# A gated delta layer on one core: v turned by VectorE and transfers, the residual's product kept in PSUM, and new queue orders

## The chip, the cores and the metric

The kernel runs on one core of one Trainium2 chip. The metric is the device time of one execution in microseconds (us). The engines run side by side, each from its own queue in its own order: TensorE (PE in the profile, its weight loads PEld), VectorE (DVE), ScalarE (ACT), GpSimd (POOL) and SyncE (SP), which issues every transfer (DMA). They wait for one another by semaphores. Matrix products land in PSUM, here eight banks of 128x512 f32; everything else an engine works on lies in SBUF.

## The reference

All of it is f32. A layer norm, a gated delta rule over 16 sequences of 256 tokens and 32 heads of 64, a residual, and a small feed-forward part:

```python
qkvz = (hidden_states @ w_qkvz.T)            # then q, k, v through a causal conv of 4 taps
g = -jnp.exp(A_log) * jax.nn.softplus(a + dt_bias);  beta = jax.nn.sigmoid(b)
q = _l2norm(q) * DK ** (-0.5);  k = _l2norm(k)
def step(Sstate, xs):
    q_t, k_t, v_t, g_t, b_t = xs
    Sstate = Sstate * jnp.exp(g_t)[..., None, None]
    kv = jnp.einsum('bhk,bhkv->bhv', k_t, Sstate)
    delta = (v_t - kv) * b_t[..., None]
    Sstate = Sstate + k_t[..., :, None] * delta[..., None, :]
    o_t = jnp.einsum('bhk,bhkv->bhv', q_t, Sstate)
    return (Sstate, o_t)
o = o * lax.rsqrt(var + EPS) * norm_weight * jax.nn.sigmoid(z)
x = x + _layernorm(o.reshape(Bsz, Sl, VDIM) @ w_out.T)
x = x + _layernorm((jax.nn.silu(gate) * up) @ w_down.T)
```

## The kernel before

Three stages follow each other: the first norms and the gates (up to about 110 us), the delta rule, and the feed-forward part (from about 3000 us).

The delta rule is cut into 64 steps: 8 groups of 4 heads by 8 spans of 512 tokens. A step holds 16 chunks of 64x64 (G = 16) for each of the two halves of 64 partitions. Its recurrence is written chunk by chunk: within a chunk the triangular system is inverted, between chunks a state of 64x64 is carried, over 4 chunks a sequence (c = 0 to 3); every step starts with an empty state. The inverse is built from 16x16 blocks on VectorE (`substitute`, 15 columns, each a product and a subtraction), joined on TensorE to 32 (`join16_inner`, `join16_outer`) and to 64 (`join_inner`, `join_outer`).

The steps run in a software pipeline four deep. The program is written out in turns: in turn t an engine works on the steps `s[0]` = t, `s[1]` = t - 1, `s[2]` = t - 2 and `s[3]` = t - 3, and the function `turn` of each engine is an order written out by hand. There are 67 turns; the pace of the stage is the length of a turn. Engines take a step at different depths: what GpSimd and SyncE call `s[3]` is not the step that TensorE calls `s[3]`.

What TensorE does for a step, in the names of the code:

- `project(m, s, bank)`: 8 projections into one of the banks 0 to 3 (2 k, 2 q, 2 v, 2 z), each two products of 128x128 by 128x512; `xT` is the input, in two buffers. ScalarE and VectorE take the taps out of the bank (`first_tap`, `tap_product`, `conv`); GpSimd adds q's taps (`add_tap`).
- `k_tokens` and `v_tokens` (both through `tokens`, line 1266): k and v are turned from channels by tokens to tokens by channels, as products with a unit matrix, a half of the step in each call. `scale_k` and `scale_v` (lines 1073 and 1077) take the result out of PSUM and scale it into `kt` and `v_r`.
- `scores`: k against k and q, four calls. `matrices` (lines 1089 and 1090) multiplies them with the decays into `a_mat` and `p_t`.
- for each chunk c: `key_state` (the state against k, line 1332), `residual` on VectorE (lines 1100 and 1103: the product with `b_eg` goes to `rhs`, then v minus it to `rhs`), `solve` (line 1342), `delta_out` on ScalarE (line 894), `advance` (line 1352), `new_state` on VectorE (line 1113), and `output` (lines 1365 and 1367). `decay_state` (line 1106) prepares `s_dec` for `new_state`.
- `sum_squares`, then after VectorE's `combine` and `gated` the output product `project_out`, added up by `accumulate`.

SyncE's transfers in a turn: `units_out` (16x16 blocks of `a_mat` to DRAM, 4 transfers of 32x16x32), `load_gates`, `units_in` (back as `a_un`, one row a block), then after `turn_units` on ScalarE `z_out` and `z_back`, `x_out` and `x_back`, and `load_x` for `xT`. A transfer that waits holds up those behind it in SyncE's queue.

The banks: before, each use of the banks 0 to 3 is written out as a number; bank 4 holds the chunk recurrence, bank 5 the joins, banks 6 and 7 the output.

Of the kernel before, what the change touches and what calls it, by code (L numbers as in the profile page):

```python
# [18 lines left out]
def gated_delta_sandwich(nc, x, w_qkvz, w_ba, conv_w, a_log, dt_bias, norm_w, w_out, w_gu, w_dn,  # L19
                         c_ident, c_masks, c_ones, c_eye, out):  # L20
    F32 = mybir.dt.float32
    ALU = mybir.AluOpType
# [3 lines left out]
    P = 128  # L26
# [4 lines left out]
    TB = 512  # L31
# [23 lines left out]
    with ctx:  # L55
# [37 lines left out]
        xT = [sb(f"xT{i}", [P, HT, TB]) for i in range(2)]  # L93
# [31 lines left out]
        x_row = sb("x_row", [P, G, C])  # L125
        p16 = sb("p16", [P, G, W2])
# [15 lines left out]
        class Own:  # L142


            def __init__(self, eng, s):
                self.eng, self.s, self.n = eng, s, 0
# [9 lines left out]
            def turn(self):  # L156
                if self.n:
                    self.need(self.n)
                    self.eng.sem_clear(self.s)
                    self.n = 0  # L160
# [17 lines left out]
        x_T_in = [sem(f"x_T_in{i}") for i in range(2)]  # L178
# [6 lines left out]
        with ExitStack() as s1:  # L185
# [45 lines left out]
            with nc.Block() as block:  # L231
                @block.sync
                def _(sync):
# [51 lines left out]
                    sp.dma_start(xT[0][:, :, :].rearrange("p h t -> p (h t)"), xT_d[0]).then_inc(x_T_in[0], 16)  # L285
# [253 lines left out]

        def flat(t):  # L540
            return t[:, :, :].rearrange("p a b -> p (a b)")

        wgu = [[flat(xT[0]), flat(xT[1])], [flat(w_two[1])[:, 0:INTER], flat(w_two[1])[:, INTER:2 * INTER]]]
# [16 lines left out]
        with ExitStack() as s2:  # L560
# [5 lines left out]
            abs_done = sem2("abs_done")  # L566
            cols_done = sem2("cols_done")
            comb_done = {i: sem2(f"comb_done{i}") for i in (0, 1,)}
            conv_done = {i: sem2(f"conv_done{i}") for i in (0, 1, 4, 5,)}
            deca_done = sem2("deca_done")  # L570
            delta_done = {i: sem2(f"delta_done{i}") for i in (0, 1, 2, 3,)}
# [9 lines left out]
            mats_done = {i: sem2(f"mats_done{i}") for i in (0, 1,)}  # L581
# [8 lines left out]
            qg_done = {i: sem2(f"qg_done{i}") for i in (1,)}  # L590
            rhs_done = {i: sem2(f"rhs_done{i}") for i in (1, 2, 3,)}
            rk_done = sem2("rk_done")
            score_full = {i: sem2(f"score_full{i}") for i in (0, 1, 2,)}
            sdec_done = {i: sem2(f"sdec_done{i}") for i in (2,)}
# [4 lines left out]
            sub_done = {i: sem2(f"sub_done{i}") for i in (0, 1, 2, 3, 4, 5,)}  # L599
            sumk_done = {i: sem2(f"sumk_done{i}") for i in (0,)}  # L600
            tap_added = {i: sem2(f"tap_added{i}") for i in (0, 1, 2, 3, 4, 5,)}
            tap_done = {i: sem2(f"tap_done{i}") for i in (0, 1, 2, 4, 5,)}
            tap_prod = {i: sem2(f"tap_prod{i}") for i in (3, 4, 5,)}
            usq_done = {i: sem2(f"usq_done{i}") for i in (0, 1,)}
            var_log = {i: sem2(f"var_log{i}") for i in (0, 1,)}
            vr_done = {i: sem2(f"vr_done{i}") for i in (0,)}
            vtok_full = {i: sem2(f"vtok_full{i}") for i in (0, 1,)}
# [6 lines left out]
            z_clamped = {i: sem2(f"z_clamped{i}") for i in (1,)}  # L614
# [1172 lines left out]
```

## Time and profile before

| | us |
|---|---|
| median of 3 runs | 3383.96 |
| lowest, highest | 3382.12, 3391.8 |
| the profiled execution | 3383.12 |
| its span, first to last instruction | 3381.2 |
| PE busy in the span | 3202.0 |
| DVE busy | 2463.0 |
| ACT busy | 1749.5 |
| POOL busy | 1094.8 |

The page is read from the top: which engine is busy for nearly the whole span, then whether that share is even over it. The groups of instructions by line tell what such an engine does and what ended its idle time. A row of the timeline has a start, a duration, the instruction, and in brackets the idle time ahead of it with what ended it. Starts of neighbouring rows tell what a block of pipelined instructions costs; its duration is a little longer, since blocks overlap.

### The profile page before, as it was taken

The page shows a single profiled execution, that of the slowest core. Times are in us where ns is not written, and L with a number is a line of the kernel's source. Part 1 is how long each engine was busy: PE and PEld are TensorE (multiplying, and loading weights), DVE is VectorE, ACT ScalarE, POOL GpSimd, SP SyncE. Part 2 cuts the span into 40 slices and gives each one's busy share as a digit, 9 for nine tenths or more (in the row PEclk, how much of TensorE's full clock was granted, in tenths as well). Part 3 has the DMA queues.
Part 4 walks back from the last instruction along what each step waited for, and adds up shares of the span by engine and source line. Part 5 has one row for each costly group of instructions (what it writes and reads, how often), then busy time and mean ns, then how long its engine had stood idle before and what let it go on. Part 6 is the DMA issues. An engine that isn't in the chain of part 4 may idle for free. (4 is left out here: it accounts for less than half of the span.)

```text
span 3381.2 us, 116979 instructions
## 1 busy us (share of the span) xinstructions
PE 3202.0 (95%) x51008; PEld 2181.8 (65%) x51008; DVE 2463.0 (73%) x5802; ACT 1749.5 (52%) x3306; POOL 1094.8 (32%) x904
## 2 busy tenths in 40 slices
PE   6799999999999999999999999999999999879998
PEld 3466666666666666666666666666666666645554
DVE  6677777777777777777777777777777777645554
ACT  5455555555555555555555555555555555433332
POOL 1443443333343443333343443333343343200000
PEclk8899999999999999999999999999999999989999
DMA  5233233222333222222332223222232223200000
GB/s 144 57 53 64 47 51 52 44 63 52 53 53 68 44 50 53 58 49 52 52 68 51 46 49 62 51 49 50 53 68 53 48 47 52 56 33 25 19 19 19
DMA packets 757483, 175.67 MB, mean 52 GB/s; under 512 B 707568, under 2 KB 728432, under 8 KB 755824
## 3 DMA queue, kind: packets, MB, share of 16 engines
q1 hardware_dynamic: 756976, 168.19, 26.2%
q8 instruction: 406, 6.65, 0.8%
q14 instruction: 101, 0.83, 0.1%
HBM read 120.13 MB, written 39.58 MB: 47 GB/s over the span
## 5 line engine op out<-in xcount | busy, mean ns | idle before, releaser
L1257 PE MATMUL bank<-xT,w_sb 128*128 128x512 f32 x2048 | 1018.7, 621 | 9.9 <-PEq L506 5.2
L741 POOL TENSOR_TENSOR kq<-kq,product 128x510 f32<-128x510 f32 (+2 forms) x384 | 445.0, 1165 | 882.8 <-ACT kq L829 597.2
L1257 PEld LDWEIGHTS bank<-xT,w_sb 128*128 128x128 f32 x2048 | 349.5, 190 | 295.5 <-issue 251.7
L1042 DVE SCALAR_TENSOR_TENSOR kq<-bank,cw,kq 128x510 f32<-128x510 f32 (+2 forms) x384 | 286.7, 747 | 163.0 <-ACT kq L829 149.3
L729 POOL TENSOR_TENSOR dec_a<-gcrow,gcb 128x1024 f32<-128x1024 f32 x64 | 121.8, 1903 | 832.2 <-DMA gcb<-gcb_d 832.2
L1042 DVE SCALAR_TENSOR_TENSOR v_c<-bank,cw,v_c 128x510 f32<-128x510 f32 (+2 forms) x384 | 285.3, 743 | 9.0
L1060 DVE TENSOR_TENSOR x_un<-x_un,prod_un 128x15 f32<-128x15 f32 (+7 forms) x960 | 258.3, 269 | 32.9
L1056 DVE TENSOR_TENSOR prod_un<-a_un,x_un 128x15 f32<-128x15 f32 (+7 forms) x960 | 255.8, 266 | 30.1 <-DMA a_un<-a_d 3.2
L1285 PE MATMUL bank<-kq 64*64 64x128 f32 x4096 | 270.3, 271 | 4.4 <-DVE v_c L1042 2.1
L1389 PE MATMUL bank<-wo,u_sq 128*128 128x256 f32 x1024 | 260.9, 399 | 3.5 <-DVE u_sq L1125 3.5
L835 ACT ACTIVATE product<-bank,cw 128x512 f32<-128x512 f32 x384 | 246.7, 703 | 0.0
L1367 PEld LDWEIGHTS bank<-p_t,delta 64*64 64x64 f32 x4096 | 215.1, 136 | 47.0 <-issue 47.0
L1367 PE MATMUL bank<-p_t,delta 64*64 64x64 f32 x4096 | 243.3, 220 | 0.0
L1365 PEld LDWEIGHTS bank<-q_g,state 64*64 64x64 f32 x3072 | 179.6, 134 | 95.4 <-issue 95.4
L1285 PEld LDWEIGHTS bank<-kq 64*64 64x64 f32 x4096 | 229.8, 133 | 7.6 <-issue 7.6
L894 ACT COPY delta<-bank 128x256 f32<-128x256 f32 x256 | 94.7, 370 | 244.3 <-PE bank L1342 244.3
L1389 PEld LDWEIGHTS bank<-wo,u_sq 128*128 128x128 f32 x1024 | 188.1, 193 | 34.4 <-DVE u_sq L1125 4.3
L1365 PE MATMUL bank<-q_g,state 64*64 64x64 f32 x3072 | 205.8, 226 | 1.1 <-ACT delta L894 1.1
L829 ACT ACTIVATE kq<-bank,cw 128x512 f32<-128x512 f32 x256 | 170.0, 690 | 62.4 <-PE bank L1257 62.4
L1342 PE MATMUL bank<-rhs,z_t 64*64 64x64 f32 x3072 | 128.3, 222 | 72.6 <-DVE rhs L1103 72.6
L1342 PEld LDWEIGHTS bank<-rhs,z_t 64*64 64x64 f32 x3072 | 107.3, 135 | 127.0 <-issue 127.0
L1089 DVE TENSOR_TENSOR a_mat<-bank,dec_a 128x256 f32<-128x256 f32 x256 | 106.4, 415 | 107.2 <-PE bank L1285 106.9
(170 smaller groups left out, 6004.7 us busy)
## 6 DMA issues: line engine op xcount, KB each, us to landing
xT<-xT_d SPq DMA_DIRECT2D x64, 512.0 KB, 3.8
gcrow<-gcrow_d SPq DMA_DIRECT2D x128, 256.0 KB, 4.5
a_d<-a_mat SPq DMA_DIRECT2D x256, 64.0 KB, 2.1
z_t<-z_d SPq DMA_DIRECT2D x256, 64.0 KB, 2.5
w_sb<-in_w_qkvz SPq DMA_DIRECT2D x8, 1024.0 KB, 5.9
x_un<-eye_un SPq DMA_DIRECT2D x64, 128.0 KB, 3.7
a_un<-a_d SPq DMA_DIRECT2D x64, 128.0 KB, 4.7
z_d<-t_un SPq DMA_DIRECT2D x64, 128.0 KB, 3.0
```

Of the source, the lines that this page charges most:

```text
L741: nc.gpsimd.tensor_tensor(t[:, :, d:SEQ], t[:, :, d:SEQ], prod[:, :, 0:SEQ - d], ALU.add).then_inc(tap_added[i], 1)
L829: ins = nc.scalar.activation(dst, bank[:, :], ACT.Identity, scale=cw_two[m.grp % 2][:, s * TAPS + TAPS - 1:s * TAPS + TAPS])
L835: ins = nc.scalar.activation(products[i % 4], bank[:, :], ACT.Identity, scale=cw_two[m.grp % 2][:, w:w + 1])
L1042: ins = nc.vector.scalar_tensor_tensor(t[:, :, d:SEQ], src[:, :, 0:SEQ - d], cw_two[m.grp % 2][:, w:w + 1], t[:, :, d:SEQ], ALU.mult, ALU.add)
L1056: own.need(own.mark(nc.vector.tensor_tensor(prod, a_un[:, j + 1:B, j:j + 1].broadcast_to([P, rows, wid]), x_un[:, j:j + 1, 0:wid].broadcas ...
L1060: ins = nc.vector.tensor_tensor(rest, rest, prod, ALU.subtract)
L1257: ins = nc.tensor.matmul(bank[:, :], w_two[m.grp % 2][:, h, s * P:(s + 1) * P], xT[m.par][:, h, :], start=(h == 0), stop=(h == HT - 1))
L1285: ins = nc.tensor.matmul(bank[half, i * P:(i + 1) * P], kq[half, k, s // 2, t0:t0 + C], kq[half, k:q + 1:q - k, s // 2, t0:t0 + C], start= ...
L1342: ins = nc.tensor.matmul(banks[4][half, 256 + i * C:256 + (i + 1) * C], z_t[m.par][half, g, :], rhs[half, i, :] if c else v_r[m.par][half, ...
L1365: nc.tensor.matmul(o, state[c % 2][half, i, :], q_g[m.par][half, g, :], start=True, stop=False)
L1367: ins = nc.tensor.matmul(o, delta[half, i, :], p_t[m.par][half, g, :], start=(c == 0), stop=True)
L1389: ins = nc.tensor.matmul(bank[:, t * HID:(t + 1) * HID], u_sq[:, a, (2 * k + t) * P:(2 * k + t + 1) * P], wo[m.grp % 2][:, a, :], start=(a ...
```

## The change

1. `v_tokens` is gone from TensorE. `turn_v` on VectorE transposes 32x32 blocks of v from `v_c` into a new buffer `v_x`, a half of the step in each call; eight transfers (`v_turned`) lay the blocks out in `v_r`; `scale_v` then works in place on `v_r` in SBUF. It runs a turn later than before.
2. `residual` writes its product back into its PSUM bank and subtracts from there.
3. `substitute` is called column by column, 15 parts in place of 6, with other work between them; it starts in one turn and ends in the next.
4. `xT` has one buffer in place of two (`product` takes over as the buffer of a weight in the last stage). `decay_state` now always signals.
5. The banks 0 to 3 are used in a ring that turns by two each step.
6. Every engine's order in a turn is new.

```diff
-        xT = [sb(f"xT{i}", [P, HT, TB]) for i in range(2)]
+        xT = sb("xT", [P, HT, TB])
+        v_x = sb("v_x", [P, G, C])
+        def ring(m, place):
+            return banks[(18 * m.off + place) % 4]
...
+                    def v_turned(m):
+                        for h in range(2):
+                            for f in range(2):
+                                for t in range(2):
+                                    r, q = D * h + W2 * t, D * h + W2 * f
+                                    sp.dma_start(v_r[m.par][r:r + W2, :, W2 * f:W2 * f + W2], v_x[q:q + W2, :, W2 * t:W2 * t + W2]) \
+                                        .then_inc(v_f_in, 16)
...
+                    def turn_v(m, a):
+                        ins = nc.vector.transpose(v_x[:, a * GP:(a + 1) * GP, :].rearrange("p g c -> p (g c)"), v_c[:, a, :])
+                        if a in vx_done:
+                            ins.then_inc(vx_done[a], 1)
...
-                    def scale_v(m, a, bank):
+                    def scale_v(m, a):
                         g = slice(a * GP, (a + 1) * GP)
-                        ins = nc.vector.tensor_tensor(v_r[m.par][:, g, :], bank[:, :].rearrange("p (g c) -> p g c", c=C), col(br[:, g]).broadcast_to([P, GP, C]), ALU.mult)
+                        ins = nc.vector.tensor_tensor(v_r[m.par][:, g, :], v_r[m.par][:, a * GP:(a + 1) * GP, :], col(br[:, g]).broadcast_to([P, GP, C]), ALU.mult)
...
                     def residual(m, c):
-                        own.need(own.mark(nc.vector.tensor_tensor(
-                            rhs[:, :, :], banks[4][:, 0:256].rearrange("p (a j) -> p a j", j=C),
-                            col(b_eg[m.par][:, c:G:NCH]).broadcast_to(four), ALU.mult)))
-                        nc.vector.tensor_tensor(rhs[:, :, :], grp(v_r[m.par], c), rhs[:, :, :], ALU.subtract).then_inc(rhs_done[c], 1)
+                        ks = banks[4][:, 0:256].rearrange("p (a j) -> p a j", j=C)
+                        own.need(own.mark(nc.vector.tensor_tensor(ks, ks, col(b_eg[m.par][:, c:G:NCH]).broadcast_to(four), ALU.mult)))
+                        nc.vector.tensor_tensor(rhs[:, :, :], grp(v_r[m.par], c), ks, ALU.subtract).then_inc(rhs_done[c], 1)
...
-                    def v_tokens(m, a, bank):
-                        ins = tokens(v_c[:, :, :], a, bank)
-                        ins.then_inc(vtok_full[a], 1)
```

What stands where now is shown for three places. Some semaphores are shown under the name of an earlier stage that used the same one.

TensorE, the part of a turn from `sum_squares` to `advance` of chunk 0; before, with `v_tokens` as `bank<-masks,v_c` and one early projection:

```order
L1382 MATMUL bank1<-u_sq,ones 128x512 [waits sq_added1]
L1382 MATMUL bank2<-u_sq,ones 128x512 [waits sq_added0]
L1314 MATMUL bank5<-z_t1,a_mat1 32x32 [waits z16_done]
L1314 MATMUL bank5<-z_t1,a_mat1 32x32 x31
L1266 MATMUL bank3<-masks,v_c 64x64 [waits mats_done1]
L1266 MATMUL bank3<-masks,v_c 64x64 x15
L1266 MATMUL bank0<-masks,v_c 64x64 [waits mats_done0]
L1266 MATMUL bank0<-masks,v_c 64x64 x15
L1323 MATMUL bank5<-p1,x_top 32x32 [waits p1_done,xtop_done]
L1323 MATMUL bank5<-p1,x_top 32x32 x31
L1257 MATMUL bank1<-xT1,w_sb1 128x512 [waits x_T_in1,comb_done1]
L1257 MATMUL bank1<-xT1,w_sb1 128x512
```

And now:

```order
L1355 MATMUL bank5<-p16,x_row 48x32 x31
L1432 MATMUL bank2<-u_sq,ones 128x512 [waits sq_added0]
L1310 MATMUL bank3<-xT,w_sb1 128x512 [waits x_T_in,mats_done2]
L1310 MATMUL bank3<-xT,w_sb1 128x512
L1310 MATMUL bank0<-xT,w_sb1 128x512 [waits mats_done0]
L1310 MATMUL bank0<-xT,w_sb1 128x512
L1364 MATMUL bank5<-z_t1,a_mat1 32x32 [waits z16_done]
L1364 MATMUL bank5<-z_t1,a_mat1 32x32 x31
L1439 MATMUL bank1<-wo1,u_sq 128x256 [waits og_done0]
L1439 MATMUL bank1<-wo1,u_sq 128x256 x3
L1373 MATMUL bank5<-p1,x_top 32x32 [waits p1_done,xtop_done]
```

The 32 products of `v_tokens` are gone, and two projections of the next step (`bank<-xT,w_sb`) stand between the joins, where they wait for nothing that is computed in the turn but the matrices and the input.

VectorE, ahead of the second `residual`; before, the columns 9 to 14 of the substitution stand in one piece (the last five rows of it here) ahead of it:

```order
L1056 TENSOR_TENSOR prod_un<-a_un,x_un 128x28 [waits soft]
L1060 TENSOR_TENSOR x_un<-x_un,prod_un 128x2x14 [waits soft]
L1056 TENSOR_TENSOR prod_un<-a_un,x_un 128x15 [waits soft]
L1060 TENSOR_TENSOR x_un<-x_un,prod_un 128x15 [waits soft]
L1100 TENSOR_TENSOR rhs<-bank4,b_eg1 128x256 [waits ks_full2]
L1103 TENSOR_TENSOR rhs<-v_r1,rhs 128x256 [waits soft]
```

And now:

```order
L1149 TENSOR_TENSOR state<-bank,s_dec 128x256 [waits st_full1,sdec_done1]
L1116 TENSOR_TENSOR v_r<-v_r,cols 128x512 [waits v_f_in]
L1089 TENSOR_TENSOR prod_un<-a_un,x_un 128x15 [waits tok_ready]
L1093 TENSOR_TENSOR x_un<-x_un,prod_un 128x15 [waits tok_ready]
L1144 TENSOR_TENSOR s_dec<-state,e_end 128x256 [waits state_done1]
L1140 TENSOR_TENSOR bank<-bank,b_eg 128x256 [waits ks_full2]
L1141 TENSOR_TENSOR rhs<-v_r,bank 128x256 [waits tok_ready]
```

Between `new_state` of chunk 1 and the second `residual` only one column, one `scale_v` and one `decay_state` are left.

SyncE, one turn; before:

```order
L671 DMA a_d<-a_mat1 32x16x32 [waits mats_done0]
L671 DMA a_d<-a_mat1 32x16x32 x3
L659 DMA gcrow<-gcrow_d 64x2x512 [waits qg_done1]
L659 DMA gcrow<-gcrow_d 64x2x512
L662 DMA gcb<-gcb_d 128x32
L676 DMA a_un<-a_d 128x16x16 [waits a_d_out]
L679 DMA z_d<-t_un 128x16x16 [waits alpha_done]
L687 DMA x_d<-x_un 64x16x16
L684 DMA z_t1<-z_d 32x16x32 [waits z_d_out]
```

And now:

```order
L669 DMA gcrow<-gcrow_d 64x2x512 [waits qg_done1]
L669 DMA gcrow<-gcrow_d 64x2x512
L672 DMA gcb<-gcb_d 128x32
L681 DMA a_d<-a_mat 32x16x32 [waits mats_done0]
L681 DMA a_d<-a_mat 32x16x32 x3
L686 DMA a_un<-a_d 128x16x16 [waits a_d_out]
L709 DMA v_r<-v_x 32x16x32 [waits vx_done1]
L709 DMA v_r<-v_x 32x16x32 x7
L697 DMA x_d<-x_un 64x16x16 [waits sub_done14]
L689 DMA z_d<-t_un 128x16x16 [waits gc_ready]
L694 DMA z_t<-z_d 32x16x32 [waits z_d_out]
```

The gates' three transfers now go ahead of the blocks of `a_mat`, v's eight stand behind the load of `a_un`, and the two results of the substitution behind those.

## Rows read from the trace of the kernel before

**Rows 1.** The page: the span and each engine's busy time.

```profile
span 3381.2 us, 116979 instructions
PE 3202.0 (95%) x51008; PEld 2181.8 (65%) x51008; DVE 2463.0 (73%) x5802; ACT 1749.5 (52%) x3306; POOL 1094.8 (32%) x904
```

**Rows 2.** Busy time by windows: stretch, length, PE, PEld, DVE, ACT, POOL, clock, DMA.

```profile
200.00:2600.00 2400.00, 2335.86 (x41365) 1624.82 (x41361) 1845.83 (x4300) 1318.78 (x2478) 910.32 (x751) 1.00 0.29 54
```

**Rows 3.** PE's groups by line: count, busy us, mean ns, idle before and releaser.

```profile
L1266 PE MATMUL bank<-masks,v_c 64*64 64x64 f32 x4096 | 134.0, 220 | 0.7 <-issue 0.6
L1342 PE MATMUL bank<-rhs,z_t 64*64 64x64 f32 x3072 | 128.3, 222 | 72.6 <-DVE rhs L1103 72.6
```

**Rows 4.** DVE's timeline: the same instruction (`tail`) in two turns that follow each other.

```profile
1419.33 0.18 DVE L1035 TENSOR_TENSOR cols<-gcrow,gcb 128x16 f32<-128x16 f32 x1
...
1463.71 0.18 DVE L1035 TENSOR_TENSOR cols<-gcrow,gcb 128x16 f32<-128x16 f32 x1
```

**Rows 5.** PE's timeline, the middle of that turn (`output` stands in the gap ahead of L1332).

```profile
1430.76 0.68 PE L1342 MATMUL bank<-rhs,z_t 64*64 64x64 f32 x16 [1.03 <-DVE rhs L1103]
...
1433.81 1.10 PE L1266 MATMUL bank<-masks,kq 64*64 64x64 f32 x32
...
1435.67 0.68 PE L1332 MATMUL bank<-state,kq 64*64 64x64 f32 x16
1436.28 1.98 PE L1257 MATMUL bank<-xT,w_sb 128*128 128x512 f32 x4
1438.20 0.68 PE L1342 MATMUL bank<-rhs,z_t 64*64 64x64 f32 x16
```

**Rows 6.** DVE's timeline ahead of the second `residual` of that turn.

```profile
1425.94 1.16 DVE L1060 TENSOR_TENSOR x_un<-x_un,prod_un 128x55 f32<-128x55 f32 x1
1427.13 1.12 DVE L1056 TENSOR_TENSOR prod_un<-a_un,x_un 128x48 f32<-128x48 f32 x1
...
1430.19 0.43 DVE L1103 TENSOR_TENSOR rhs<-v_r,rhs 128x256 f32<-128x256 f32 x1
```

**Rows 7.** POOL's timeline at the same time: two of `add_tap`.

```profile
1425.69 2.50 POOL L741 TENSOR_TENSOR kq<-kq,product 128x510 f32<-128x510 f32 x2 [10.66 <-ACT kq L829]
```

**Rows 8.** DVE's groups by line: `scale_v` and the transpose of `z_t`.

```profile
L1077 DVE TENSOR_TENSOR v_r<-bank,cols 128x512 f32<-128x512 f32 x128 | 88.5, 692 | 74.6 <-PE bank L1266 74.6
...
L1135 DVE STREAM_TRANSPOSE x_top<-z_t 128x512 f32<-128x512 f32 x64 | 44.6, 697 | 2.2 <-ACT z_t L872 2.2
```

**Rows 9.** ACT's timeline: `turn_units` of that turn.

```profile
1429.86 0.62 ACT L862 COPY t_un<-x_un 128x256 f32<-128x256 f32 x1 [4.25 <-DVE x_un L1060]
```

**Rows 10.** SyncE's timeline: start, issue time and count of each kind of transfer.

```profile
1404.34 1.96 SPq L671 DMA_DIRECT2D a_d<-a_mat  x4
1406.41 2.37 SPq L659 DMA_DIRECT2D gcrow<-gcrow_d  x2
1408.83 0.60 SPq L662 DMA_DIRECT2D gcb<-gcb_d  x1
1409.61 0.39 SPq L676 DMA_DIRECT2D a_un<-a_d  x1
1430.57 0.37 SPq L679 DMA_DIRECT2D z_d<-t_un  x1
...
1433.63 3.20 SPq L684 DMA_DIRECT2D z_t<-z_d  x4
```

**Rows 11.** The page's transfers: count, KB each, median us from issue to landing.

```profile
a_d<-a_mat SPq DMA_DIRECT2D x256, 64.0 KB, 2.1
z_t<-z_d SPq DMA_DIRECT2D x256, 64.0 KB, 2.5
...
a_un<-a_d SPq DMA_DIRECT2D x64, 128.0 KB, 4.7
```

**Rows 12.** PE's timeline after the last projections: two waits, for ACT's hand-over and a join.

```profile
2937.34 0.68 PE L1352 MATMUL bank<-delta,kt 64*64 64x64 f32 x16 [0.56 <-ACT delta L894]
...
2970.66 1.12 PE L1342 MATMUL bank<-v_r,z_t 64*64 64x64 f32 x16 [7.11 <-ACT z_t L887]
```

More of the change, by code:

```diff
@@ L145, in __init__ @@
             def __init__(self, eng, s):
[L146 removed]
+                self.eng, self.s, self.n, self.turns = eng, s, 0, 0
             def mark(self, ins):
@@ L156, in turn @@
             def turn(self):
+                self.turns += 1
                 if self.n:
@@ L176, in wait @@
                 eng.wait_ge(s, value)
-        x_T_in = [sem(f"x_T_in{i}") for i in range(2)]
+        x_T_in = sem("x_T_in")
         sp_gate = sem("sp_gate")
@@ L617, in gated_delta_sandwich @@
             z_in = sem2("z_in")
+            z_log = {i: sem2(f"z_log{i}") for i in (1,)}
             zoff_done = sem2("zoff_done")
@@ L873, in outer16_out @@
                         ins.then_inc(z16_done, 1)
+                        if m.off == STEPS - 1:
+                            first_deviations(0)
                     def inner_out(m):
@@ L1053, in substitute @@
                             prod = prod_un[:, 0:rows * wid].rearrange("u (i j) -> u i j", j=wid)
-                            if j > columns[0]:
+                            if j and last_sub[1] == own.turns:
                                 own.need(last_sub[0])
@@ L1143, in turn @@
                     def turn(s):
+                        if s[3]:
+                            wait_for(dve, ks_full[1], s[3], 1)
+                            residual(s[3], 1)
                         if s[1]:
-                            wait_for(dve, gc_in, s[1], 48)
-                            tail(s[1])
+                            wait_for(dve, tap_done[1], s[1], 1)
+                            conv(s[1], 1, ring(s[1], 1))
                         if s[2]:
-                            wait_for(dve, sub_done[0], s[2], 1)
-                            substitute(s[2], 1, range(2, 4))
-                            wait_for(dve, sub_done[1], s[2], 1)
-                            substitute(s[2], 2, range(4, 6))
+                            substitute(s[2], 10, range(10, 11))
+                            substitute(s[2], 11, range(11, 12))
                         if s[3]:
+                            decay_state(s[3], 1)
+                        if s[2]:
+                            substitute(s[2], 12, range(12, 13))
+                            substitute(s[2], 13, range(13, 14))
+                        if s[3]:
+                            wait_for(dve, sdec_done[1], s[3], 1)
                             wait_for(dve, st_full[1], s[3], 1)
@@ L1394, in turn @@
                     def turn(s):
+                        if s[3]:
+                            wait_for(pe, delta_done[0], s[3], 1)
+                            advance(s[3], 0)
                         if s[1]:
-                            wait_for(pe, vr_done[0], s[1], 1, back=1)
-                            project(s[1], 6, banks[0])
+                            wait_for(pe, tap_prod[2], s[1], 1)
+                            project(s[1], 7, ring(s[1], 2))
+                        if s[3]:
+                            wait_for(pe, state_done[0], s[3], 1)
+                            key_state(s[3], 1)
+                        if s[1]:
+                            project(s[1], 3, ring(s[1], 3))
                         if s[3]:
@@ L1416, in turn @@
                         if s[1]:
-                            project(s[1], 3, banks[3])
-                            wait_for(pe, z_exp[0], s[1], 1)
-                            k_tokens(s[1], 1, banks[0])
+                            wait_for(pe, z_exp[1], s[1], 1)
+                            k_tokens(s[1], 1, ring(s[1], 2))
                         if s[3]:
+                            output(s[3], 1)
                             wait_for(pe, rhs_done[2], s[3], 1)
```

425 lines of the change are left out of this document (218 added, 207 removed).

## The prediction, made before the changed kernel was run

> **What bounds the kernel now.** I read the page first: PE is busy for 3202.0 of 3381.2 us, the next engine, DVE, for 2463.0 [rows 1]. The windows next, since a share over the whole span hides its stages: from 200 to 2600 us PE is busy for 2335.86 of 2400, at full granted clock, DVE for 1845.83 and POOL for 910.32 [rows 2]. So the delta rule, most of the span, is bound by PE. Its pace is the length of a turn: the same instruction of `tail` comes at 1419.33 and at 1463.71, so a turn is 44.38 us [rows 4], and 64 steps of it are 2840 us. The window holds 2400 / 44.38 = 54.1 turns; its idle 64.1 us are 1.19 a turn, and PE's work is 44.38 - 1.19 = 43.19 a turn. Where the idle time sits, the groups say: 72.6 us of it, 1.13 a turn, come before `solve`, released by `rhs` of DVE [rows 3]; in the turn that I followed that is one wait of 1.03 us at the second `solve` [rows 5]. Just ahead of it DVE ran columns 9 to 14 of the substitution in one piece, and two of its instructions took 1.16 and 1.12 us instead of about 0.2 [rows 6], beside two additions of POOL that began at 1425.69 and ran for 2.50 [rows 7].
>
> **v off TensorE.** The products on `v_c` are 134.0 us of PE's busy time, 2.09 a turn [rows 3], and nothing hides them: PE is the bound and their idle time is 0.7. They go whole. 43.19 - 2.09 leaves **41.10 us of work a turn**. No product is added, so that is the floor: 64 x (44.38 - 41.10) = 210 us less if every wait went too.
>
> **v on VectorE.** Two transposes of 128x512 come in, each about the 697 ns of the one on `z_t`; `scale_v` was 692 from PSUM [rows 8] and, reading SBUF, I take it for the same, since `rhs<-v_r,rhs` and the product from PSUM ahead of it cost alike when nothing disturbs (0.43 [rows 6]). DVE has 1845.83 / 54.1 = 34.1 us of work a turn now [rows 2], so 35.5 after, 85% of a turn of 41.7. It isn't the bound, but it has 6 us to spare in place of 10. In the new order the transposes stand between `combine` and `conv` of the next step; ahead of the gated product stands one of them, 0.7 us. Laid out with the durations of these rows, the gated products end about 0.8 us before PE's `project_out` wants them.
>
> The row of two stretched instructions shows two-input work on SBUF standing still for one addition of POOL. The Trainium skill, SBUF — State Buffer, "Who interferes with whom", says that a VectorE instruction with two SBUF inputs contends with a GpSimd instruction that reads SBUF, and one with a single SBUF input doesn't. By that rule this change cuts both ways: the residual's subtraction (now from PSUM) is freed, the transposes are safe, and `scale_v` becomes exposed. What it makes of the time: `scale_v` twice a turn, at worst behind one addition of 1.25 us each (half of the 2.50 [rows 7]), 2.5 us of DVE. That would still leave DVE at 38 of 41.7.
>
> **v's transfers.** Eight a turn, of 32x16x32, the shape of `z_t<-z_d`: four of those are issued in 3.20 us [rows 10], so eight take up to 6.4, and land after 2.5 [rows 11]. They start when both transposes are done, about 34 us into the turn (counted from `advance` of chunk 0), so they have landed by 43; `scale_v` comes at 50.6, 9 us into the next turn. 7 us of cover: cost nothing. Behind them in SyncE's queue stands `x_out`, which waits for the last column at about 10 us of the next turn and is not held up.
>
> **The substitution in pieces, the residual in PSUM.** A chunk's hand-over must fit between PE's blocks. The block costs come from the starts of neighbours: a projection 1.92 (1436.28 to 1438.20), a chunk's product 0.61, `k_tokens` or `output` 0.93 (two in 1433.81 to 1435.67) [rows 5]. With them the new turn is: `advance` of chunk 0 at 0, `key_state` 1 at 2.5, `solve` 1 at 5.6, `advance` 1 at 8.1, `key_state` 2 at 10.6, `solve` 2 at 13.2, `advance` 2 at 14.7, `key_state` 3 at 17.2, `solve` 3 at 19.8, `output` 3 at 21.3. `residual` takes 0.87 (two of 0.43 [rows 6]) and a hand-over on either side, 1.1 in all after the 0.68 of `key_state`: `solve` 1 has 1.2 us to spare, `solve` 2 and 3 have 0.8. ACT's `delta` costs 0.56 from product to product [rows 12]: 0.3 is left at chunks 2 and 3, 1.2 at chunk 1. On DVE the second `residual` now has behind `new_state` 1 only a `scale_v`, one column and a `decay_state`, 1.5 us, which end 0.7 before `key_state` 2 does. So the old wait of 1.03 goes. The product written to PSUM in place of SBUF has no row of DVE's; I take 0, bounded by ±0.1 a piece (a quarter of 0.43 either way), which the 0.8 covers.
>
> **SyncE's order.** (a) `a_un`: its blocks now stand behind the gates. The gates are asked for when `scale_q` is done, at 24.5, and take 2.37 + 0.60; then the blocks 1.96 + 2.1 to land, then `a_un` 4.7 [rows 10, 11]: 24.5 + 2.97 + 1.96 + 2.1 + 4.7 = 36.2. DVE wants it at 36.6 and can bear it until about 38.4, because it would otherwise wait for `project_out`. (b) `z_t`: from `turn_units` (0.62 [rows 9]) to `z_d` 0.1, to the first `z_t` 3.06, 3.20 of issue, 2.5 to land [rows 10, 11], 9.0 us counting from the start of the last issue. It starts at 12.9, ends at 21.9; `join16_inner` is due at 23.3. 1.4 to spare, where the old turn had about 3. Both chains hold on paper and are the thinnest places: (a) has 2.2, (b) 1.4. (c) `xT` in one buffer: loaded behind `x_back`, landed by 27, wanted at 29.
>
> **Sum.** No wait in that layout is above zero. But such slacks are small beside what issues scatter, so I keep half of the old idle time: 0.6 a turn, between 0 and 1.2. A turn: 41.10 + 0.6 = 41.7. 64 x (44.38 - 41.7) = 171.5; 3381.2 - 171.5 = 3209.7, and 1.9 between span and time give 3211.6; the median lies 0.8 above the profiled execution: **3212**. Ends: idle 0 gives 3174, idle 1.2 gives 3251. Filling and draining the pipeline keep their turns; the drain has a wait of 7.11 at a join [rows 12] which may go or grow: ±7, in the ends.
>
> **Rivals.**
> 1. *New waits eat a good part.* DVE with 6 us to spare in small gaps, `scale_v` behind POOL, and `gated` or `z_t` late: each of the three places misses by about 0.8. Idle 2.5 a turn, a turn of 43.6, 3331. For it: every slack that I found is below 1.5 us. Against it: these misses are not added up where PE catches one wait behind another.
> 2. *Slower: the order of SyncE.* If `a_un` lands late, the substitution starts late, and with it the state of the next step. The gates go first now, and v's 4096 packets share the engines with `a_un`. It decides from 38.4 on: every us beyond is a us a turn, and the kernel gets slower from 38.4 + 3.3 = 41.7, that is 5.5 us later than my 36.2. At 42.5: 4.1 idle, a turn of 45.2, 3436. Against it: `a_un` is issued before v's transfers.
> 3. *The turn isn't bound where I think*, and another loop (DVE, then POOL, then the gates) paces it as before: about 3384.
> 4. *The floor and a shorter drain*: below 3174.
>
> **Chances.** Forecast (3174 to 3251) 0.66, rival 1 0.20, rival 2 0.06, rival 3 0.05, rival 4 0.03. The range 3172 to 3300 takes the forecast and the lower third of rival 1. What a measurement can tell from no change is about 0.3%, 10 us. Faster 0.89, same 0.04, slower 0.07.
>
> **What would show it.** The turn by the starts of `tail`: 41.7 (43.6 by rival 1, above 44.4 by rival 2). No products on `v_c`; PE idle before `solve` well below 72.6; DVE near 35.5 a turn, and the two stretched instructions gone. `scale_v` at 0.69, or longer beside POOL. Waits of DVE for `a_un` at zero (rival 2: several us), of `join16_inner` for `z_t` at zero. I am wrong if PE's busy time falls by less than 134, or if its idle time in the steady part rises above 1.2 a turn.

## The result, and the profile after

The changed kernel takes 3152.19 us (median of 4 runs, 3146.08 to 3162.45), the kernel before 3387.41 (4 runs, 3382.12 to 3391.8). The ratio is 0.9309, with a 95% interval of 0.9278 to 0.934. The forecast was 3212, and the time lies below its range, which began at 3172: the direction held, but the turn became shorter than the floor that I had worked out.

The page, as [rows 1]:

```profile
span 3147.4 us, 109678 instructions
PE 3025.3 (96%) x46912; PEld 2041.3 (65%) x46912; DVE 2404.0 (76%) x5930; ACT 1764.0 (56%) x3306; POOL 1116.3 (35%) x904
```

The same stretch by windows, as [rows 2] (stretch, length, PE, PEld, DVE, ACT, POOL, clock, DMA share, GB/s):

```profile
200.00:2600.00 2400.00, 2386.63 (x41504) 1647.10 (x41505) 1956.29 (x4817) 1453.47 (x2705) 1014.35 (x822) 1.00 0.40 71
```

PE's group that used to wait, as [rows 3]; the group on `v_c` is gone:

```profile
L1392 PE MATMUL bank<-rhs,z_t 64*64 64x64 f32 x3072 | 128.5, 221 | 7.5 <-DVE rhs L1141 7.5
```

`tail` in two turns that follow each other on DVE, as [rows 4]:

```profile
1433.77 0.17 DVE L1067 TENSOR_TENSOR cols<-gcrow,gcb 128x16 f32<-128x16 f32 x1
...
1474.33 0.17 DVE L1067 TENSOR_TENSOR cols<-gcrow,gcb 128x16 f32<-128x16 f32 x1
```

An undisturbed turn is 40.56 us, where it was 44.38. PE's idle time in the long stretch fell from 64.1 to 13.4 us, and PE is still the bound. Over all 63 intervals between the 64 tails the mean went from 44.40 to 40.80: 63 x 3.60 = 226.7 us of the 233.8 by which the span is shorter. The rest is 1.4 us at the start and 5.7 behind the last tail. The gain is thus in the turn, and the question is what it consists of: 3.82 us, of which 1.03 were the wait of [rows 5], so PE's own work in a turn fell by 2.79. The products on `v_c` explain 2.01 (their block in that turn lasted from 1451.30 to 1453.31). **0.78 us a turn** went that neither the bracketed wait nor a removed product explains. 0.21 of it belongs to the old wait after all: the `k_tokens` block ahead of it took 1430.76 - 1428.59 - 1.03 = 1.14 us where its like took 0.93 [rows 5], since blocks overlap at their ends and a wait's bracket begins only when the last product is through. 0.57 remain.

Part of PE's timeline in that turn, to be read beside [rows 5]. First the middle, where each block follows the last one with no wait in brackets:

```profile
1434.83 0.68 PE L1382 MATMUL bank<-state,kq 64*64 64x64 f32 x16
1435.44 1.98 PE L1310 MATMUL bank<-xT,w_sb 128*128 128x512 f32 x4
1437.36 0.68 PE L1417 MATMUL bank<-p_t,delta 64*64 64x64 f32 x16
1437.87 0.63 PE L1392 MATMUL bank<-rhs,z_t 64*64 64x64 f32 x16
1438.44 1.98 PE L1310 MATMUL bank<-xT,w_sb 128*128 128x512 f32 x4
1440.35 0.68 PE L1402 MATMUL bank<-delta,kt 64*64 64x64 f32 x16
...
1460.70 3.60 PE L1310 MATMUL bank<-xT,w_sb 128*128 128x512 f32 x8
1464.23 1.20 PE L1364 MATMUL bank<-z_t,a_mat 32*32 32x32 f32 x64
```

The last two rows hold the hint. A projection alone between blocks of small tiles costs 1.92 from start to start (1438.44 to 1440.35). Two side by side cost 3.53 (1460.70 to 1464.23), not 3.83.

### The profile page after: what moved, and what is told of

It reads as the page before. It is cut to its first block and busy times, and to the rows that moved or that the text cites. A ratio compares the mean times of both kernels' runs of the same rounds, so it can differ in the third digit from the quotient of the medians.

```text
span 3147.4 us, 109678 instructions
## 1 busy us (share of the span) xinstructions
PE 3025.3 (96%) x46912; PEld 2041.3 (65%) x46912; DVE 2404.0 (76%) x5930; ACT 1764.0 (56%) x3306; POOL 1116.3 (35%) x904
## 5 line engine op out<-in xcount | busy, mean ns | idle before, releaser
L1310 PE MATMUL bank<-xT,w_sb 128*128 128x512 f32 x2048 | 995.8, 614 | 16.4 <-DVE kq L1074 9.1
L1310 PEld LDWEIGHTS bank<-xT,w_sb 128*128 128x128 f32 x2048 | 359.3, 190 | 355.6 <-issue 311.4
L765 POOL TENSOR_TENSOR kq<-kq,product 128x510 f32<-128x510 f32 (+2 forms) x384 | 437.0, 1144 | 105.2 <-ACT kq L861 90.6
L1335 PE MATMUL bank<-kq 64*64 64x128 f32 x4096 | 278.7, 270 | 3.4 <-DVE p_t L1129 2.0
L1089 DVE TENSOR_TENSOR prod_un<-a_un,x_un 128x15 f32<-128x15 f32 (+7 forms) x960 | 215.6, 225 | 63.4 <-DMA a_un<-a_d 45.5
L865 ACT ACTIVATE product<-bank,cw 128x512 f32<-128x512 f32 x384 | 256.8, 688 | 2.1 <-PE bank L1310 2.1
L769 POOL TENSOR_SCALAR z_tmp<-z_tmp 128x512 f32<-128x512 f32 x128 | 78.5, 613 | 472.6 <-ACT z_tmp L855 467.1
L1093 DVE TENSOR_TENSOR x_un<-x_un,prod_un 128x15 f32<-128x15 f32 (+7 forms) x960 | 202.8, 211 | 32.9
L778 POOL TENSOR_TENSOR q_g<-kq,gcrow 128x512 f32<-128x512 f32 x128 | 188.4, 1492 | 0.9 <-PE bank L1417 0.5
L1382 PEld LDWEIGHTS bank<-state,kq 64*64 64x64 f32 x3072 | 112.0, 135 | 97.5 <-issue 97.5
```

What stands on the lines that cost most here:

```text
L765: nc.gpsimd.tensor_tensor(t[:, :, d:SEQ], t[:, :, d:SEQ], prod[:, :, 0:SEQ - d], ALU.add).then_inc(tap_added[i], 1)
L778: ins = nc.gpsimd.tensor_tensor(q_g[m.par][:, a * GP:(a + 1) * GP, :], half_of(m, 1)[:, a, :].rearrange("p (g c) -> p g c", c=C), gcrow[:, ...
L865: ins = nc.scalar.activation(products[i % 4], bank[:, :], ACT.Identity, scale=cw_two[m.grp % 2][:, w:w + 1])
L1089: own.need(own.mark(nc.vector.tensor_tensor(prod, a_un[:, j + 1:B, j:j + 1].broadcast_to([P, rows, wid]), x_un[:, j:j + 1, 0:wid].broadcas ...
L1093: ins = nc.vector.tensor_tensor(rest, rest, prod, ALU.subtract)
L1310: ins = nc.tensor.matmul(bank[:, :], w_two[m.grp % 2][:, h, s * P:(s + 1) * P], xT[:, h, :], start=(h == 0), stop=(h == HT - 1))
```

## The experiments

A turn below is the undisturbed one, the length that comes most often between the starts of `tail`, where a kernel has one. The four times of the new kernel lie 16 us apart, so a single run tells no difference under about 10 us; the turn is finer. Two kernels with a pair of added products and one with an early join were run 4 times each, the others once. The diffs are shortened: guards and waits are left out. The profile counts each f32 product of TensorE as two instructions, so a projection of two products reads x4.

### v alone, in the old order

```diff
-        for i in range(GP):
+        for i in range(chunks):     # v_tokens passes 1, k_tokens GP
```

> The kernel before, its orders unchanged; each of the two calls that turn v on PE makes one of its eight chunks (seven eighths of v's turning are left out, so v_r holds stale data). Theory A (PE's work sets the turn, and v's products cost their busy time): the turn falls by 7/8 of 2.01 = 1.76 us, from 44.38 to 42.6, the time by about 113 to 3272. Theory B (they cost more than their busy time through what stands around them): the turn falls by clearly more, 2.2 or more. Theory C (DVE or a transfer catches up): by less than 1.3.

Measured: 3384.01 us (before 3389.39 beside it). Seven eighths of the block are gone and the time hardly moves. PE's timeline where `v_tokens` stood, then windows of the same place (as [rows 2]):

```profile
1454.02 0.45 PE L1266 MATMUL bank<-masks,v_c 64*64 64x64 f32 x8
1455.44 1.51 PE L1323 MATMUL bank<-p,x_top 32*32 32x32 f32 x64 [0.97 <-ACT p L878]
1456.88 3.27 PE L1257 MATMUL bank<-xT,w_sb 128*128 128x512 f32 x4
```

```profile
1452.00:1455.00 3.00, 2.46 (x75) 1.52 (x73) 2.73 (x5) 2.02 (x4) 0.00 (x0) 1.00 0.54 79
1455.00:1458.00 3.00, 2.56 (x66) 2.01 (x67) 1.97 (x4) 2.45 (x5) 0.00 (x0) 0.68 0.32 83
1458.00:1461.00 3.00, 3.00 (x21) 1.41 (x20) 0.10 (x1) 0.99 (x3) 0.00 (x0) 0.75 1.03 149
```

Two things eat the 1.76 us. The products on `v_c` had covered ScalarE's hand-over of the join (`p`, line 878), and now PE waits 0.97 for it; `join_outer`'s group waits 62.8 us over the run. With the 0.21 that a wait costs beyond its bracket this gives 44.38 - 1.76 + 0.97 + 0.21 = 43.80, and 43.80 is what an otherwise undisturbed turn takes. And behind that wait the granted clock drops, in 22 of the 54 turns of the long stretch: the projection takes 3.27 us in place of 1.98, and the turn about 45.4. So my sentence "They go whole" was true only of an order in which something else covers the join.

To see whether that cover is the reason, the next kernel, with the same single chunk, also moves `join_outer`, `solve` 0 and `advance` 0 one block further back each, so that a projection stands ahead of the join, and ScalarE's `outer_out` behind a `first_tap`:

```diff
-    outer_out(s[3])                  # ScalarE
     first_tap(s[1], 1, banks[1])
+    outer_out(s[3])
...
-    join_outer(s[2])                 # TensorE
     project(s[0], 1, banks[1])
-    solve(s[2], 0)
+    join_outer(s[2])
     project_out(s[3], 1, banks[2])
-    advance(s[2], 0)
+    solve(s[2], 0)
     project_out(s[3], 0, banks[3])
+    advance(s[2], 0)
     key_state(s[2], 1)
```

> The kernel before with v's products cut to one chunk in eight, as b_v_eighth, and with the blocks after the inner join in another order on PE: projection, outer join, output product, solve 0, output product, advance 0, key_state 1 (on ACT the tap of that projection goes ahead of the outer join's copy). Theory cover (v's products hid ACT's copy between the joins, and without them PE idles 0.98 there and its clock falls in about half the turns): the wait at the outer join is gone, a new one of about 0.6 stands at key_state 1; undisturbed turns of 43.4 in place of 43.80, no turns of 45.4 with a lower granted clock, time about 3320 in place of 3384. Rival (the old order is bound elsewhere too, DVE or a transfer): still 43.8 or more, 3370 to 3390.

Measured: 3334.38 us (before 3381.05). The wait at the join is gone. A new one stands at the first `key_state`, since `advance` now comes directly ahead of it:

```profile
1433.67 0.68 PE L1351 MATMUL bank<-delta,kt 64*64 64x64 f32 x16
1434.97 0.68 PE L1331 MATMUL bank<-state,kq 64*64 64x64 f32 x16 [0.62 <-DVE state L1114]
```

No single length stands out among its turns; most lie between 42.3 and 45.3, and their mean is 43.47, 0.93 under the 44.40 of before. The kernel gains 47 us where the first one gained 5. In the long stretch the clock drops once, where it dropped 22 times without cover. Cover brings back about half of the 1.76; the new wait of 0.62, with the 0.21 beside it, is the other half: 44.38 - 1.76 + 0.83 = 43.45.

### v back on TensorE, in the new order

```diff
+    v_tokens(s[1], 1, ring(s[1], 3))   # PE, ahead of join16_outer
     join16_outer(s[2])
+    v_tokens(s[1], 0, ring(s[1], 0))
...
-    turn_v(s[1], 0)                    # DVE, likewise turn_v(s[1], 1) and SyncE's v_turned
```

> The changed kernel with v turned on PE again, in the new order (two calls beside the join of 16; scale_v from PSUM, no transposes, no transfers of v). Theory A (v's own part of the gain is its work, the rest the order): turn 40.56 + 2.0 = 42.6, time 3280. Theory B (most of the gain needs v off PE): above 43.5, 3338 or more.

Measured: 3267.55 us, a turn of 42.46. The order and all else but v is therefore worth 3389.39 - 3267.55 = 122 us, and v's move, in that order, 115 us. By the turn they are 1.92 and 1.90 us. The two halves are alike in size, where my sum gave v 134 us and the order 38 (0.6 x 64).

```profile
200.00:2600.00 2400.00, 2387.89 (x43218) 1680.23 (x43220) 1817.80 (x4480) 1390.25 (x2580) 971.30 (x784) 1.00 0.29 56
```

PE is idle for 12.1 us of 2400 with v on it, 13.4 without: v's move touched no wait.

### Is PE still the bound?

The chunk loop of `k_tokens` runs twice, the same products again into the same place:

```diff
-        for i in range(GP):
+        for i in 2 * list(range(GP)):
```

> The changed kernel with k's turning on PE done twice, the same 32 products a step again into the same bank. If PE sets the turn of the changed kernel: 40.56 + 1.86 = 42.4, time about 3271. If DVE or SyncE's chain set it, under 41.5.

Measured: 3281.11 us, a turn of 42.43: 1.87 more, what the doubled blocks cost themselves. What was put on PE came back whole in the turn, so no other engine paces the new kernel.

### The old wait, undone by itself

```diff
-    substitute(s[2], 5, range(12, 15))
     wait_for(dve, ks_full[2], s[3], 1)
     residual(s[3], 2)
+    substitute(s[2], 5, range(12, 15))
```

> The kernel before with one move: the second residual goes ahead of columns 12 to 14 of the substitution on DVE. Theory A (the wait of 1.03 ahead of the second solve is the order of DVE, and it costs its row): turn 44.38 - 1.03 = 43.35, time 3318. Theory B (a wait also costs the emptying of PE around it, about 0.2, the block ahead of it took 1.14 in place of 0.93): turn 43.15, time 3305. Theory C (the later t_un turns into a wait of the join): no gain.

Measured: 3419.19 us and a turn of 44.95, slower than before, though the wait for `rhs` fell from 72.6 to 7.6 us. Two other waits took its place. PE's timeline, then a row of ScalarE's and one of DVE's:

```profile
1451.07 0.68 PE L1354 MATMUL bank<-delta,kt 64*64 64x64 f32 x16 [0.69 <-ACT delta L894]
1452.57 1.15 PE L1268 MATMUL bank<-masks,kq 64*64 64x64 f32 x32 [0.82 <-DVE kq L1042]
```

```profile
1448.87 0.63 ACT L862 COPY t_un<-x_un 128x256 f32<-128x256 f32 x1 [5.04 <-DVE x_un L1060]
1450.12 2.31 DVE L1042 SCALAR_TENSOR_TENSOR kq<-bank,cw,kq 128x510 f32<-128x510 f32 x3 [0.95 <-ACT kq L829]
```

The root is ScalarE. Its copy `t_un` waits for the last column of the substitution, which now ends later, and behind `t_un` in its queue stand the taps for `conv` and `delta`. So `delta` comes 0.69 too late for PE; DVE is idle for 0.95 ahead of `conv`, and PE waits 0.82 for the `k_tokens` that `conv` feeds. In the kernel before, ScalarE is idle for 272.1 us in all ahead of `t_un`; in the new one, whose order has the last column done by then, for 2.0. The wait could be taken away only together with ScalarE's order.

How much of the old wait did the finer split of the substitution take away? Here columns 10 to 14 stand in one piece again in the new kernel:

```diff
-    substitute(s[2], 10, range(10, 11))
...
     scale_v(s[2], 1)
-    substitute(s[2], 14, range(14, 15))
+    for j in range(10, 15):
+        substitute(s[2], j, range(j, j + 1))
```

> The changed kernel with columns 10 to 14 of the substitution in one piece ahead of the second residual on DVE, as the kernel before had columns 9 to 14. If the interleaving of single columns took the old wait away: PE waits again at the second solve, 0.3 to 1.0 a turn, turn 40.9 to 41.6, time 3171 to 3215. If the freedom from POOL's additions or PE's new order did it: turn 40.56, within 0.3% of 3152.

Measured: 3171.53 us, a turn of 40.96, 0.40 more. In the long stretch PE waits 61 times for `rhs`, nearly always for about 0.2 and at the second `solve`; the sum, and one of them in the timeline:

```profile
PE bank L1386 <- DVE rhs L1141: 13.0, 61, 1.1
```

```profile
1458.13 0.33 PE L1411 MATMUL bank<-p_t,delta 64*64 64x64 f32 x4
1458.63 0.68 PE L1386 MATMUL bank<-rhs,z_t 64*64 64x64 f32 x16 [0.17 <-DVE rhs L1141]
```

The bracket says 0.17, but from start to start it is 0.50. The same two blocks in the new kernel begin 0.12 apart (1445.14 and 1445.26), so the wait costs 0.38, and again 0.21 of that is lost overlap. That is nearly the whole of the 0.40, but only a third of the 1.24 that the old wait of 1.03 cost with its 0.21. In this kernel no addition of POOL runs beside the columns ahead of that `residual`, so the two instructions of [rows 6], 1.16 and 1.12 us, take 0.2 like the others. That is about 1.9 us less on DVE, so the missing collision with POOL may well be the larger part. It is read from the two traces and not shown by a run, since none puts the additions back.

### Where the other 0.57 us come from

If what costs is the border between products over all 128 rows and products on tiles of 64x64 or 32x32, then a pair of tiny products between two neighbouring projections must cost more than the same pair within a run of small ones. One function, two places:

```diff
+    def extra():
+        for h in range(2):
+            half = slice(D * h, D * h + D)
+            nc.tensor.matmul(banks[4][half, 256:256 + C], eye64[half, :], eye64[half, :], start=True, stop=True)
     project(s[0], 0, ring(s[0], 1))
+    extra()                            # first kernel: here; second: ahead of scores(s[1], 0)
     project(s[0], 2, ring(s[0], 2))
```

> The changed kernel with one more pair of 64x64 products (its result is not used) between the two projections that stand side by side. Theory border (a run of 128-row products broken by small ones costs the borders, the pair of projections took 3.53 where two alone take 3.83): the turn grows by 0.3 or more, from 40.56 to 40.9, the time by 20 us or more. Theory work: by 0.03 to 0.06, under 4 us.

> The same pair of 64x64 products between two small blocks (the inner join of 16 and the last scores). Both theories: the turn grows by under 0.1, the time by under 6 us.

Measured: between the projections 3172.42 us (4 runs, ratio 0.9365, 0.9351 to 0.9379) and a turn of 41.02, 0.46 more. Within the run 3151.08 us (4 runs, ratio 0.9304, 0.9283 to 0.9324) and 40.68, 0.12 more, a little above the 0.1 that I had allowed. The kernel with them between:

```profile
1437.28 1.88 PE L1310 MATMUL bank<-xT,w_sb 128*128 128x512 f32 x4
1439.09 0.33 PE L1331 MATMUL bank<-masks 64*64 64x64 f32 x4
1439.35 1.98 PE L1310 MATMUL bank<-xT,w_sb 128*128 128x512 f32 x4
1441.26 1.20 PE L1369 MATMUL bank<-z_t,a_mat 32*32 32x32 f32 x64
```

From 1437.28 to 1441.26 the pair takes 3.98, where it took 3.53. The products are the same in both kernels: of the 0.46, 0.34 is the break in the run of large blocks. The Trainium skill, TensorEngine Tiling (Array Packing), "Key Properties", says that a change of tiling mode drains TensorE. These rows agree with it.

The weight loads of the new kernel show where a run pays. The run from 1459.74 to 1464.23 is the second half of `sum_squares` and the pair of projections:

```profile
1459.74 0.30 PEld L1432 LDWEIGHTS bank<-u_sq,ones 128*128 128x128 f32 x2
1460.28 0.19 PEld L1310 LDWEIGHTS bank<-xT,w_sb 128*128 128x128 f32 x1 [0.24 <-issue]
...
1463.28 0.19 PEld L1310 LDWEIGHTS bank<-xT,w_sb 128*128 128x128 f32 x1 [0.24 <-issue]
1464.23 0.17 PEld L1364 LDWEIGHTS bank<-z_t,a_mat 32*32 32x32 f32 x6 [0.76 <-issue]
```

Within the run each product's weights are loaded during the product ahead of it, and products follow each other every 0.43 us. At both ends the load waits for the old shape to finish and begins together with its own product. So the first product of the run begins 0.13 behind the last small one (small ones are about 0.02 apart), the second 0.53 behind the first in place of 0.43, and the first small product 0.52 behind the last large one. The excess is 0.11 + 0.10 + 0.09 = 0.30. Whether the array must be empty or only the load can't run ahead, no run separates. A smaller gap stands between small tiles of different size: in the kernel before, 0.12 from the last product of the inner join (1451.17, 32x32) to the first on `v_c` (1451.30, 64x64), where those of the join are 0.016 apart.

If a break costs 0.3, one break less must pay. The third kernel moves `join16_outer` ahead of both `sum_squares`, so that these and the two projections stand in one run. ScalarE's `outer16_out` and DVE's `turn_back` move up with it:

```diff
+    join16_outer(s[2])
     sum_squares(s[3], 1, ring(s[3], 1))
-    join16_outer(s[2])
     sum_squares(s[3], 0, ring(s[3], 2))
```

> The changed kernel with the outer join of 16 ahead of both sums of squares, on ACT and DVE too, so that one run of small blocks fewer stands among the 128-row ones. Theory border: turn 40.56 - 0.26 = 40.3, time down by 17 us to 3135. Rival (the row data for that join lands too late, it now comes 1 us earlier): equal or slower by up to 0.5 a turn, 3152 to 3184.

Measured: **3137.78 us** (4 runs, 3136.24 to 3141.52; ratio 0.9262, 0.9246 to 0.9277), a turn of 40.29, 0.27 less. This beats both kernels. The rival shows a little: in the long stretch PE waits 13 times for the row data, 4.7 us in all. The place in its timeline:

```profile
1454.30 1.63 PE L1354 MATMUL bank<-p,x_row 64*48 64x32 f32 x64
1455.86 1.98 PE L1431 MATMUL bank<-u_sq,ones 128*128 128x512 f32 x4
1457.68 3.60 PE L1309 MATMUL bank<-xT,w_sb 128*128 128x512 f32 x8
1461.21 1.20 PE L1363 MATMUL bank<-z_t,a_mat 32*32 32x32 f32 x64
```

### The residual in PSUM, both ways

The new kernel with the old form; the other run is the reverse, the new form in the kernel before:

```diff
-    ks = banks[4][:, 0:256].rearrange("p (a j) -> p a j", j=C)
-    own.need(own.mark(nc.vector.tensor_tensor(ks, ks, col(b_eg[m.par][:, c:G:NCH]).broadcast_to(four), ALU.mult)))
-    nc.vector.tensor_tensor(rhs[:, :, :], grp(v_r[m.par], c), ks, ALU.subtract).then_inc(rhs_done[c], 1)
+    own.need(own.mark(nc.vector.tensor_tensor(
+        rhs[:, :, :], banks[4][:, 0:256].rearrange("p (a j) -> p a j", j=C),
+        col(b_eg[m.par][:, c:G:NCH]).broadcast_to(four), ALU.mult)))
+    nc.vector.tensor_tensor(rhs[:, :, :], grp(v_r[m.par], c), rhs[:, :, :], ALU.subtract).then_inc(rhs_done[c], 1)
```

> The kernel before with the residual's product written back into its PSUM bank, nothing else. On the path at the second solve only; if the second instruction of the residual no longer waits for POOL: the row 0.64 in the third residual becomes 0.42, which has cover. Expected turn 44.38 within 0.1, time within 0.3% of before. If the write to PSUM is dearer by 0.1, turn 44.5.

> The changed kernel with the residual's product in SBUF again. If its place in PSUM carries part of the gain (POOL's additions run beside the first and second residual now): solve waits for rhs, turn up by 0.3 to 1.2, 3171 to 3225. If the cover of 0.8 holds: turn 40.56, time within 0.3% of 3152.

Measured: in the kernel before 3391.62 us (3389.91 beside it), in the new one 3146.73: no difference in the time either way, with turns of 44.38 and 40.56. The durations do change. DVE's groups of the new kernel with the product in SBUF, then those of the new kernel as it is:

```profile
L1142 DVE TENSOR_TENSOR rhs<-v_r,rhs 128x256 f32<-128x256 f32 x192 | 130.7, 681 | 6.6
L1116 DVE TENSOR_TENSOR v_r<-v_r,cols 128x512 f32<-128x512 f32 x128 | 87.9, 686 | 0.0
```

```profile
L1140 DVE TENSOR_TENSOR bank<-bank,b_eg 128x256 f32<-128x256 f32 x192 | 83.1, 433 | 64.9 <-PE bank L1382 60.4
L1141 DVE TENSOR_TENSOR rhs<-v_r,bank 128x256 f32<-128x256 f32 x192 | 80.8, 421 | 6.7
...
L1116 DVE TENSOR_TENSOR v_r<-v_r,cols 128x512 f32<-128x512 f32 x128 | 106.2, 830 | 0.0
```

Written into the bank, the product costs 433 ns (422 into SBUF in the kernel before); my bounds were 0.1 us either way. The subtraction with both inputs in SBUF is stretched to a mean of 681, with one in PSUM it takes 421. Relieved of that collision, `scale_v`, which also reads twice from SBUF, meets POOL instead: 63 of its 128 instructions now run beside POOL's product for `dec_p` and take 968 on average, which makes the mean 830 in place of 686. That is the trade that the Trainium skill, SBUF — State Buffer, "Who interferes with whom", describes: a VectorE instruction with two inputs in SBUF contends with a GpSimd instruction that reads SBUF, one with a single such input doesn't. The trace agrees: 183 of the 192 subtractions from PSUM run beside POOL, and all 192 take 420 to 422. It makes no difference to the time, because DVE has room for both.

### SyncE's order

```diff
+    wait_for(sp, mats_done[0], s[3], 1)
+    units_out(s[3])
     load_gates(s[2])
-    wait_for(sp, mats_done[0], s[3], 1)
-    units_out(s[3])
```

> The changed kernel with SyncE's order of before at one place: the blocks of a_mat go out ahead of the gates. a_un lands up to 1 us earlier, DVE's wait for it (45.5 us) falls below 20. If that wait has cover: time within 0.3% of 3152. If it carried some of PE's idle time: down by up to 10 us; if the gates come too late for POOL: up.

Measured: 3170.24 us, 18 more, and DVE's waits for `a_un` did not fall (48.5 us, 45.5 in the new kernel). My account of that wait fell: it isn't the gates ahead of the blocks. What did change is POOL: its first decay (`dec_a` from the gates) comes later, and it and the additions behind it run beside the substitution. 62 of the products below run beside that decay, for 1.03 us on average where most others take about 0.2, and 69 beside an addition, for 1.12 (45 in the new kernel, for 0.59). The product of the substitution in this kernel, then in the new one:

```profile
L1090 DVE TENSOR_TENSOR prod_un<-a_un,x_un 128x15 f32<-128x15 f32 (+7 forms) x960 | 332.6, 346 | 66.6 <-DMA a_un<-a_d 48.5
```

```profile
L1089 DVE TENSOR_TENSOR prod_un<-a_un,x_un 128x15 f32<-128x15 f32 (+7 forms) x960 | 215.6, 225 | 63.4 <-DMA a_un<-a_d 45.5
```

That is 117 us of stretched products on DVE, and PE's waits for `rhs` double to 14.4 us. PE's idle time in the long stretch is 27.5 us in place of 13.4. The turns have no undisturbed length any more: most lie between 40.0 and 42.5, three between 43.6 and 46.5, and their mean is 41.13, 0.33 above that of the new kernel.

## Why the forecast was too high

- **v off TensorE.** Right in kind, 2.09 us a turn forecast. The block was 2.01, and in the new order the move is worth 1.90 and 115 us. It needed the cover that the new order gives: in the old order leaving out seven eighths of it brought 5 us, less than a run can tell.
- **The floor.** This is the step that failed: "41.10 us of work a turn. No product is added, so that is the floor". The turn came out at 40.56, which is 0.54 less, 34 us over 63 turns. I took PE's work as the sum of its blocks wherever they stand. The runs show that a block's cost depends on its neighbours: a break in a run of 128-row blocks costs about 0.3 us (0.34 when one is put in, 0.27 when one is taken out). The new order has 10 such runs a turn where there were 11, and that can be read from the order before anything runs. Of the 0.57 us this explains about 0.3. From start to start over the turn, the 0.57 is made of 0.30 less in the eight projections, 0.25 in the four `solve` blocks (the one at 1445.26, now between blocks of small tiles, takes 0.46, the one at 1438.20 of the kernel before, between projections, 0.61), 0.10 in `key_state`, 0.08 in `output` and 0.05 in `advance`, against 0.11 more in `scores` and the joins of 16 and 0.10 more in `sum_squares`, which was split. Beyond the one run saved, most of it thus lies in small blocks that now stand among small ones; no run separates these terms. The sum made smaller slips beside that: it took the mean idle time of 1.19 off an undisturbed turn that holds only 1.03, it took 2.09 for the block on `v_c`, whose instructions overlap, where 2.01 goes, and it knew nothing of the 0.21 that a wait costs beyond its bracket.
- **The idle time.** I kept 0.6 us a turn, between 0 and 1.2. It was 13.4 us in 2400 / 40.80 = 58.8 turns, 0.23, and an undisturbed turn has none, as the layout had said. I halved the old idle time out of distrust, with no row behind the half: (0.6 - 0.23) x 63 = 23 us too much. With the 34 of the floor that is 57 of the 60 us between forecast and result.
- **The hand-overs of chunks 1 to 3** fit between the blocks: `rhs` fell from 72.6 to 7.5 us, `delta` holds PE for 3.3 in all.
- **v on VectorE.** Transposes 701 ns (forecast 697). DVE is busy for 1956.29 / 58.8 = 33.3 us a turn, not 35.5. I left out what the new places save, chiefly in the substitution, whose 1920 instructions took 514.1 us and now take 418.4. Of them 127 took over 0.3 us, two a turn as in [rows 6]; now 43 do. `scale_v` has a mean of 830 where 692 was taken, within the bound that I drew from POOL.
- **v's transfers.** Eight were issued in 6.59 us in the turn followed (forecast 6.4), and no engine waits for them.
- **SyncE's order.** Both chains held. In the turn followed, the last `z_t` is issued by 1451.05 and takes 2.5 to land; `join16_inner` starts at 1454.65 without a wait, 1.1 later (1.4 forecast). `a_un` does make DVE wait, 45.5 us in all, where I said none; but more than a dozen turns in which it waits 0.3 to 1.2 still take 40.56, which is what the 1.8 us of tolerance in my layout (36.6 to 38.4) said; the three with 3.3 to 3.9 take 41.5 to 42.7. It landed in 3.5 us (4.7 before), `a_d` in 3.5 (2.1 before).
- **The rivals.** Rival 2, slower by SyncE, and rival 3, another loop, are excluded by these waits and by the doubled `k_tokens`. Rival 1 fell with an idle time of 0.23 (its 3331 also lacks the 2.7 us between span and median; 3334 is meant). The time lies in the band of rival 4, which had 0.03 of the chance, but not by its means: the floor itself was 34 us too high, and the end behind the last tail is shorter by only 5.7. I gave it that little because I saw no way to shorten work that stays.

**What stays open.** PE's waits in the long stretch of the new kernel:

```profile
PE bank L1346 <- issue: 5.3, 10, 0.8
PE bank L1319 <- issue: 3.3, 8, 0.6
PE bank L1392 <- DVE rhs L1141: 2.6, 3, 0.9
```

About 9 of the 13.4 us that are left are gaps of up to 0.8 us within blocks of small tiles, marked "issue", which no wait explains; they are most of the difference between 40.56 and the mean of 40.80. Their cause was not tried. Nor is it settled why the clock drop described below came in only 22 of 54 turns, all of which have the same wait.

## What to carry to other kernels

In a kernel bound by TensorE, price a block by its neighbours as well as by its products: list the runs of blocks with one tile shape before and after (a full-row run merged or split was about 0.3 us here), and add the lost overlap, 0.21 us here, to every wait. When a wait is moved, look at what stands behind it in the queue of every engine that the late work feeds, not only the bound one's. Before work is taken off the bound engine, look up what it covers: the hand-over behind it becomes a wait, and removing one wait alone moves it to the next thin place. The move of v and the new order are worth about the same here, and v's move is worth nearly nothing in the old order.

## What the runs showed of the hardware

- Granted clock: with seven eighths of v's products gone from the old order, the clock read 0.68 and 0.75 in two windows of 3 us, so part of each was at the 1.2 GHz level, though PE was busy for 2.56 and 3.00 us of them. Ahead of it PE had run products on 32x32 tiles, a few on 64x64 (eight instructions) and then stood idle for 0.97 us. A projection took 3.27 us instead of 1.98. All 54 turns of the long stretch have that idle time, 22 the drop. In the new kernel, where the same joins are followed by blocks over 128 rows without idle time, the stretch reads 1.00.
- Borders: a pair of products on 64x64 tiles (four instructions) costs 0.12 us among small ones and 0.46 between two projections. At the ends of a full-row run the weight load begins only with its own product, inside the run 0.43 us ahead of it.
- A wait costs the turn 0.21 us more than its bracket shows, seen at a wait of 1.03 and at one of 0.17; at one of 0.97 the sum of the turn comes out with it.
- VectorE's subtraction of 128x256 with one input in PSUM takes 420 to 422 ns beside POOL's instructions or not; with both inputs in SBUF, beside POOL's product for `dec_p`, it took 1021 on average.
- A VectorE product of 128x256 written over its own input in PSUM takes 433 ns, into SBUF 422.
